# One-core gated cross-attention layer: projections' work redistributed over ScalarE, VectorE and GpSimd, k and q stored at full width, first groups' loads spread

## The chip, the cores and the metric

The kernel runs on one core of a Trainium2 chip. The metric is the device time of one execution in microseconds. The comparison is between medians of several executions; the profile is one execution of its own.

## The reference, cut to what matters

Eight sequences of 512 tokens with 256 features attend to a context of 512 tokens with 192 features, with 16 heads of 16; then an expert layer (8 experts, hidden size 1024) follows.

```
def layer(x, ctx):
    xn = (x - mean(x)) / sqrt(var(x) + 1e-5)            # per token, 256 features
    q = (xn @ Wq + bq) by heads;  k, v = (ctx @ Wk + bk), (ctx @ Wv + bv) by heads
    attn = softmax(clip(q k^T * 16**-0.5, -10000, 10000))
    x = x + tanh(g_xattn) * ((attn @ v) @ Wo + bo)
    xn = layernorm(x)
    gates = logits * (logits >= kth smallest),  logits = xn @ gate_weight.T
    return x + tanh(g_ffn) * sum over experts of gates[e] * (gelu(xn @ w1[e].T + b1[e]) @ w2[e].T + b2[e])
```

## The kernel before, in words

Three blocks of instructions follow each other; a block's engines start together, once all of them have finished the block before. The change touches the first, `build_project`, and the loads and matmul operands of the second, `build_attend`. The third, the experts, takes two thirds of the time and is not touched.

**Projections.** Each number that TensorE multiplies is split into a high part rounded to its short float32 format and a low part, and a product takes three matmuls (high by high, low by high, high by low). For each of the eight batches (of 512 tokens) x is normalised on VectorE (`layer_norm`, L392: statistics, small operations on 128x4 numbers, a square root on ScalarE, `root`, one Newton step, and at L401 the normalised x), transposed on TensorE (`turn`, L293), taken from PSUM by ScalarE (high part) and VectorE (low part, `split_x`, L419). GpSimd splits the weights (`split_weights`, L242, L245) and each batch's context (`split_ctx`, L251, L254). TensorE then makes k, q and v (L283); ScalarE and VectorE turn k and q into parts `k_hl` and `q_hl` (L354, L359, L410 to L414), 128 partitions x (part, half, 512) each, and ScalarE turns v into `v_out` (L365). Two buffers alternate by batch parity `p`. Every engine runs its own program in a fixed order, and semaphores tie them together.

**SyncE** issues every DMA of the block in one order. For each batch: the loads of x and ctxT two batches ahead (`load_x` L161, `load_ctx` L166), the stores of k and q (`store_qk`, L176), four of 256 KB each, and one store of v (`store_v`, L181, 544 KB). The k and q scratch has 33 rows for each head: a constant row, 16 high, 16 low. A store writes 16 rows of each of 8 heads, so its destination's dimensions are 8, 16, 512. After the sixth batch SyncE loads the q and k of groups 0 and 1 of batch 0 (`load_qk`, L443, eight DMAs a group, in pieces of 33 and 16, 17 and 32 rows), and then stores the last two batches. GpSimd fills all `q_st` and `k_st` tiles with 0 (L267, L268) before that.

**Attention.** A group is four heads of a batch; there are 32 groups. A head's q and k stand as 49 rows at the end of 64 partitions: constant row, and high and low parts in such an order that one matmul of 64 rows makes the three products. Scores of a group (L755) are reduced on VectorE to the least one of each row (L898), these lows are turned (L782), copied by ScalarE to `low_rows` (L1023) and sent by SyncE into the q tile's constant row (`send_lows`, L656). Then the transposed scores (L765) are made with that row, two groups later than the plain ones, exponentiated on ScalarE (L1012) and multiplied with v (L776). SyncE loads a group's q and k (`load_qk`) and v (L648) three groups ahead, each before the `send_lows` of the group after.

```
for name, tile, ready in (("k", k_hl[p], k_split), ("q", q_hl[p], q_split)):      # store_qk
    sp.wait_ge(ready, b + 1)
    rows = scratch[name][bass.ds(b, 1)].rearrange("a (k h r) t -> h r (a k) t", k=KT, r=KEPT)
```

## Time and profile before

| | |
|---|---|
| median of 3 runs | 2134.78 us (2133.43 to 2135.88) |
| profiled execution | 2128.79 us, of which its span, first to last instruction, is 2127.0 |
| mean granted TensorE clock | 0.969 of full |
| TensorE matmul busy | 1981.7 us, 93% of the span |
| VectorE, ScalarE, GpSimd busy | 1315.1, 720.6, 116.5 us |
| HBM read, written | 76.34 MB, 26.08 MB |

In the rows PE is TensorE, PEld its weight loads, DVE is VectorE, ACT ScalarE, POOL GpSimd, SPq the queue of SyncE, in which the entries are the issues of DMAs, not their transfers. Times are microseconds from the span's start. L283 is line 283 of the kernel. Matmul durations overlap, since they are pipelined.

### The profile page before, as it was taken

Reading aid. Unit: us, or ns where it says so; the run is one execution under the profiler, and the core shown is the slowest. Engines: PE = TensorE matmul, PEld = TensorE weight load, DVE = VectorE, ACT = ScalarE, POOL = GpSimd, SP = SyncE. Lnnn points to the kernel's source line nnn. Section 1 sums busy time; section 2 is a strip of 40 time slices with the busy share of each in tenths; the row PEclk is TensorE's granted clock in tenths of the full one; section 3 lists DMA queues with packets and bytes.
Section 4 is the critical chain, followed back from the end, with each engine's and each line's share of the span. In section 5 each row is a group of like instructions: output and inputs, shape, how many; then the busy total and the mean of one; then the engine's idle time right before and its main releaser. Section 6 shows DMA issues by size and latency. Waiting matters only on the chain.

```text
span 2127.0 us, 29692 instructions
## 1 busy us (share of the span) xinstructions
PE 1981.7 (93%) x9252; PEld 1433.7 (67%) x9252; DVE 1315.1 (62%) x2501; ACT 720.6 (34%) x1206; POOL 116.5 (5%) x199
## 2 busy tenths in 40 slices
PE   4748999999985999999999999999999999999998
PEld 4643333333334887788888888888888888888887
DVE  7748888888844667565555456456555555654544
ACT  2224766676661222222222222222222222222222
POOL 6300110011112000000000000000000000000000
PEclk9877999999996999999999999999999999999999
DMA  4763322222311001110110011001001000100111
GB/s 137 240 194 104 83 71 76 81 79 66 81 31 42 0 19 43 30 35 10 35 30 15 10 30 35 10 30 35 10 16 49 10 15 25 35 15 10 41 34 35
DMA packets 80071, 103.49 MB, mean 49 GB/s; under 512 B 25986, under 2 KB 44164, under 8 KB 80004
## 3 DMA queue, kind: packets, MB, share of 16 engines
q1 hardware_dynamic: 80004, 102.71, 16.5%
q8 instruction: 28, 0.46, 0.1%
q14 instruction: 39, 0.32, 0.1%
HBM read 76.34 MB, written 26.08 MB: 48 GB/s over the span
## 4 chain that ended last, share of the span: by engine, by line
PE 67%; DVE 1%; issue 0%; ACT 0%; DVEq 0%; ACTq 0%
PE ps_h L1821 34%; PE ps_y L1835 34%; DVE h_lo L2042 0%; DVE h_hi L2038 0%; DVE w_hi L1981 0%; DVE gated L2107 0%; DVE w_lo L1983 0%; DVE out_T_acc L2112 0%; ACT gelu L1941 0%; DVE w_lo L2150 0%; DVE gate L2053 0%; PE ps_h L1903 0%; DVEq L1990 0%; PE ps_h L1871 0%; DVEq L2176 0%
## 5 line engine op out<-in xcount | busy, mean ns | idle before, releaser
L1941 ACT ACTIVATE gelu<-ps_h,b 128x512 f32<-128x512 f32 x512 | 352.8, 689 | 1084.5 <-PE ps_h L1821 1003.4
L2038 DVE CAST h_hi<-gelu 128x512 fp32r<-128x512 f32 x512 | 221.0, 432 | 574.6 <-ACT gelu L1941 568.9
L1821 PE MATMUL ps_h<-x_hi,w_hi 128*128 (+1 forms) x1024 | 408.8, 399 | 10.5 <-DVE w_lo L1983 9.2
L1835 PE MATMUL ps_y<-h_hi,w_hi 128*128 128x512 f32 x1024 | 405.5, 396 | 6.0 <-DVE h_lo L2042 6.0
L1821 PE MATMUL ps_h<-x_lo,w_hi 128*128 (+1 forms) x1024 | 406.2, 397 | 0.0
L1821 PE MATMUL ps_h<-x_hi,w_lo 128*128 (+1 forms) x1024 | 405.8, 396 | 0.0
L1835 PE MATMUL ps_y<-h_hi,w_lo 128*128 128x512 f32 x1024 | 405.1, 396 | 0.0
L1835 PE MATMUL ps_y<-h_lo,w_hi 128*128 128x512 f32 x1024 | 404.8, 395 | 0.0
L2042 DVE TENSOR_TENSOR h_lo<-gelu,h_hi 128x512 fp32r<-128x512 f32 x512 | 357.3, 698 | 16.6
L898 DVE TENSOR_REDUCE low<-ps_s 128x1 f32<-128x512 f32 x512 | 322.0, 684 | 40.1 <-PE ps_s L755 38.0
L1012 ACT ACTIVATE probs_T<-ps_t 128x512 f32<-128x512 f32 x384 | 207.5, 598 | 102.6 <-PE ps_t L765 100.4
L1821 PEld LDWEIGHTS ps_h<-x_hi,w_hi 128*128 128x128 f32 x1024 | 193.1, 189 | 56.3 <-DVE w_lo L1983 9.0
L755 PE MATMUL ps_s<-k_st,q_st 64*128 64x512 f32 x512 | 207.3, 482 | 24.2 <-SPq L673 22.5
L1835 PEld LDWEIGHTS ps_y<-h_hi,w_hi 128*128 128x128 f32 x1024 | 192.7, 188 | 54.8 <-DVE h_lo L2042 6.9
L1821 PEld LDWEIGHTS ps_h<-x_hi,w_lo 128*128 128x128 f32 x1024 | 193.0, 188 | 46.7
L1821 PEld LDWEIGHTS ps_h<-x_lo,w_hi 128*128 128x128 f32 x1024 | 193.1, 189 | 46.3
L1835 PEld LDWEIGHTS ps_y<-h_hi,w_lo 128*128 128x128 f32 x1024 | 192.5, 188 | 46.9
L1835 PEld LDWEIGHTS ps_y<-h_lo,w_hi 128*128 128x128 f32 x1024 | 192.6, 188 | 45.3
L765 PE MATMUL ps_t<-q_st,k_st 64*128 64x512 f32 x512 | 191.1, 456 | 10.9 <-ACT probs_T L1012 7.8
L765 PEld LDWEIGHTS ps_t<-q_st,k_st 64*128 64x128 f32 x512 | 79.6, 188 | 135.7 <-ACT probs_T L1012 78.4
L755 PEld LDWEIGHTS ps_s<-k_st,q_st 64*128 64x128 f32 x512 | 85.4, 194 | 41.5 <-SPq L673 22.7
L776 PE MATMUL ps_o<-probs_T,v_st 128*17 128x512 f32 x768 | 104.3, 616 | 1.2 <-ACT probs_T L1012 1.2
(211 smaller groups left out, 1290.8 us busy)
## 6 DMA issues: line engine op xcount, KB each, us to landing
gate<-gates_scratch SPq DMA_DIRECT2D x64, 256.0 KB, 3.3
q_st<-q_scratch SPq DMA_DIRECT2D x64, 132.0 KB
k_scratch<-k_hl SPq DMA_DIRECT2D x32, 256.0 KB
q_scratch<-q_hl SPq DMA_DIRECT2D x32, 256.0 KB
k_st<-k_scratch SPq DMA_DIRECT2D x64, 128.0 KB
w_raw<-in_w1T SPq DMA_DIRECT2D x8, 1024.0 KB, 5.0
w_raw<-in_w2T SPq DMA_DIRECT2D x7, 1024.0 KB, 5.4
v_scratch<-v_out SPq DMA_DIRECT2D x8, 544.0 KB
```

Of the source, the lines that this page charges most:

```text
L755: pe.matmul(ps_s[BANK_OF[at]][:], q_st[g][rows, j // 2, t * P:(t + 1) * P], k_st[g][rows, j // 2, :], start=True, stop=True).then_inc(scor ...
L765: pe.matmul(ps_t[BANK_OF[at]][:], k_st[g][rows, j // 2, k * P:(k + 1) * P], q_st[g][rows, j // 2, :], start=True, stop=True).then_inc(t_in ...
L776: mm = pe.matmul(ps_o[32 * j:32 * j + VW, :], v_st[g][:, k, j, :], probs_T[k][:, j, :], start=(k == 0), stop=(k == TT - 1))
L898: dve.tensor_reduce(low[:, g % 2, column:column + 1], ps_s[BANK_OF[at]][:], AX_X, ALU.min).then_inc(low_done, 1)
L1012: act.activation(probs_T[k][:, j, :], ps_t[BANK_OF[(g * TT + k) * GROUP + j]][:], ACT.Exp, scale=-1.0).then_inc(exp_done, 1)
L1821: mm = pe.matmul(ps_h[:, j % RING, :], w[:, k, at], x[:, k, bass.ds(c * SEQ, SEQ)], start=(i == 0), stop=(i == len(parts) - 1))
L1835: mm = pe.matmul(ps_y[s][:, d, :], w[:, j, at], h[:, j % RING, :], start=(j == 0 and i == 0), stop=(j == HT - 1 and i == 2))
L1941: act.activation(gelu[:, j % GELUS, :], ps_h[:, j % RING, :], ACT.Gelu_apprx_tanh, bias=b1[p][:, j:j + 1]).then_inc(gelu_done, 1)
L2038: dve.tensor_copy(h_hi[:, j % RING, :], gelu[:, j % GELUS, :]).then_inc(h_hi_done, 1)
L2042: dve.tensor_tensor(h_lo[:, j % RING, :], gelu[:, j % GELUS, :], h_hi[:, j % RING, :].bitcast(F32), ALU.subtract).then_inc(h_ready, 1)
```

## The change

In the projections, the splits of weights and context move from GpSimd to ScalarE (high part) and VectorE (low part). The reciprocal root moves from VectorE and ScalarE to GpSimd, as the chain of small operations that the attention already has. VectorE's order changes: a batch's statistics are taken one batch earlier than its normalisation. q's high part is written straight from PSUM by ScalarE and its low part by VectorE, so `q_full` goes; the weights of q are scaled in their split. In the first batch TensorE makes k, then turns x, makes v and then q. Scratch for k and q becomes (batch, 128, 2, 2, 512), and each is stored with one DMA of 1 MB. The constant rows are no longer stored or loaded: the plain scores use 48 rows, the transposed ones 49, and the k tiles are filled with 1 (one each before the roots of batches 2 to 5), the q tiles not at all. A group's q and k are loaded in 12 DMAs of 16 rows (64 KB). The loads of groups 0 and 1 are made six at a time, behind the stores of batches 2 to 5. The loops of SyncE and GpSimd are unrolled.

```diff
+QK_PIECES = 12
...
-            def store_qk(bb, p):
+            def store(bb, p):
                 b = bb * 2 + p
                 for name, tile, ready in (("k", k_hl[p], k_split), ("q", q_hl[p], q_split)):
                     sp.wait_ge(ready, b + 1)
-                    rows = scratch[name][bass.ds(b, 1)].rearrange("a (k h r) t -> h r (a k) t", k=KT, r=KEPT)
-                    for part in range(2):
-                        for k in range(KT):
-                            sp.dma_start(rows[:, 1 + part * HDIM:1 + (part + 1) * HDIM, k], tile[:, part, k].bitcast(F32)).then_inc(stored[p], 16)
-
-            def store_v(bb, p):
-                b = bb * 2 + p
+                    sp.dma_start(scratch[name][bass.ds(b, 1)].rearrange("a p c m t -> (a p) (c m t)"),
+                                 tile[:].rearrange("p c m t -> p (c m t)").bitcast(F32)).then_inc(stored[p], 16)
                 sp.wait_ge(v_ready, b + 1)
                 sp.dma_start(scratch["v"][bass.ds(b, 1), :, :].rearrange("a p n -> p (a n)"),
                              v_out[p][:].rearrange("p t h w -> p (t h w)")).then_inc(stored[p], 16)
...
-            sp.wait_ge(fills_set, 2)
-            for i, name in enumerate(("q", "k")):
-                sp.dma_start(scratch[name].rearrange("b (h r) t -> (b h) r t", r=KEPT)[:, 0, :], const_rows[:, i, :]).then_inc(consts_moved, 16)
-            with sp.Fori(0, BATCH // 2 - 1) as bb:
-                for p in range(2):
-                    load_x(bb + 1, p)
-                    load_ctx(bb + 1, p)
-                    store_qk(bb, p)
-                    store_v(bb, p)
-
-            sp.wait_ge(fills_set, 3)
-            sp.wait_ge(consts_moved, 48)
-            sp.wait_ge(stored[0], STORES)
-            for g in range(FIRST_GROUPS):
-                load_qk(sp, scratch, keep, 0, g, first_loaded)
-            for p in range(2):
-                store_qk(BATCH // 2 - 1, p)
-                store_v(BATCH // 2 - 1, p)
-            sp.wait_ge(first_loaded, 128 * FIRST_GROUPS)
+            sp.dma_start(keep["wo"][:], io["Wo"].rearrange("(k p) n -> p k n", p=P)).then_inc(wo_loaded, 16)
+
+            def load_first(i):
+
+                g, name = i // 2, ("q", "k")[i % 2]
+                if i == 0:
+                    sp.wait_ge(stored[0], STORES)
+                if name == "k":
+                    sp.wait_ge(consts_set, 4 + g + 1)
+                load_rows(sp, scratch, keep, name, 0, g, first_loaded)
+
+            for b in range(BATCH):
+                if b + 2 < BATCH:
+                    load_x(b // 2 + 1, b % 2)
+                    load_ctx(b // 2 + 1, b % 2)
+                store(b // 2, b % 2)
+                if 2 <= b < 2 + 2 * FIRST_GROUPS:
+                    load_first(b - 2)
+            sp.wait_ge(wo_loaded, 16)
+            sp.wait_ge(first_loaded, QK_PIECES * 16 * FIRST_GROUPS)
...
-                pool.wait_ge(ctx_loaded[p], bb * 32 + 32)
-                wait(pool, v_in_psum, b - 1)
-                pool.tensor_tensor(ctx_hi[p][:], ctx_t[p][:], zero[:].rearrange("p (a b) -> p a b", a=1).to_broadcast([P, KT, SEQ]),
-                                   ALU.add).then_inc(ctx_split, 1)
-                pool.wait_ge(ctx_split, b * 2 + 1)
-                pool.tensor_tensor(ctx_lo[p][:], ctx_t[p][:], ctx_hi[p][:].bitcast(F32), ALU.subtract).then_inc(ctx_split, 1)
...
+                dev, diff, square, spread, var, first_root, root_2, scaled = (moments[:, i, :] for i in range(8))
+                done = b * 9
+                pool.wait_ge(stats_done, b + 1)
+                wait(pool, xn_ready, b - 1)
+                pool.tensor_tensor(diff, stats[:, :, 1], stats[:, :, 4], ALU.subtract)
...
+                pool.tensor_tensor(result, first_root, dev, ALU.add).then_inc(rstd_done, 1)
+
             for p in range(2):
                 pool.memset(v_out[p][:], 1.0).then_inc(ones_set, 1)
-            split_ctx(0, 1)
-            for i in range(2):
-                pool.memset(const_rows[:, i, :], float(i)).then_inc(fills_set, 1)
-
-            for s in range(GROUPS):
-                pool.memset(keep["q_st"][s][:].bitcast(F32), 0.0)
-                ins = pool.memset(keep["k_st"][s][:].bitcast(F32), 0.0)
-            ins.then_inc(fills_set, 1)
+            root(0, 0)
+            root(0, 1)
             pool.memset(keep["nan_flag"][:], 0)
-            with pool.Fori(1, BATCH // 2) as bb:
-                for p in range(2):
-                    split_ctx(bb, p)
+            for b in range(2, BATCH):
+                if b - 2 < GROUPS:
+                    pool.wait_ge(stats_done, b + 1)
+                    pool.memset(keep["k_st"][b - 2][:].bitcast(F32), 1.0).then_inc(consts_set, 1)
+                root(b // 2, b % 2)
...
+                    project_k(bb, p)
+                    if first:
+                        pe.wait_ge(ident_set, 2)
+                        turn(bb, p)
+                        values(bb, p)
+                    project_q(bb, p)
+                    if before_last(last, p, 1):
                         turn(bb + p, 1 - p)
-                    values(bb, p)
-
-            turn(0, 0)
+                    if not first:
...
+            def take_ctx(bb, p):
                 b = bb * 2 + p
-                act.wait_ge(stats_done, b * 4 + 4)
-                act.activation(std[:], meanvar[:, 1, :], ACT.Sqrt, bias=eps[:, 0:1]).then_inc(std_done, 1)
+                if isinstance(bb, int) and bb == 0:
+                    act.wait_ge(ones_set, p + 1)
+                act.wait_ge(ctx_loaded[p], bb * 32 + 32)
+                wait(act, v_in_psum, b - 1)
+                act.activation(ctx_hi[p][:], ctx_t[p][:], ACT.Copy).then_inc(ctx_hi_done, 1)
...
-                act.wait_ge(q_in_psum, b + 1)
-                wait(act, q_split, b)
-
+
+            def take_q(bb, p):
+                act.wait_ge(q_in_psum, bb * 2 + p + 1)
                 for m in range(KT):
-                    act.activation(q_full[:, m, :], ps_q[:, m, :], ACT.Identity, bias=bq_scaled[:, m:m + 1],
-                                   scale=-(HDIM ** -0.5)).then_inc(q_full_ready, 1)
+                    act.activation(q_hl[p][:, 0, m, :], ps_q[:, m, :], ACT.Identity, bias=bq_scaled[:, m:m + 1]).then_inc(q_hi_done, 1)
...
+            def statistics(bb, p):
                 b = bb * 2 + p
                 dve.wait_ge(x_loaded[p], bb * 16 + 16)
-                wait(dve, xn_ready, b)
-                mean_variance(dve, [x_t[p][:, t, :] for t in range(TT)], stats, meanvar, stats_done, b)
-                dve.wait_ge(std_done, b + 1)
-                rstd = reciprocal_root(dve, std[:], meanvar[:, 1, :], newton, newton_done, b)
+                wait(dve, rstd_done, b)
+                for t in range(TT):
+                    ins = dve.bn_stats(stats[:, t, :], x_t[p][:, t, :])
+                ins.then_inc(stats_done, 1)
+
+            def normalise(bb, p):
+                b = bb * 2 + p
+                dve.wait_ge(rstd_done, b + 1)
                 wait(dve, xT_in_psum, b - 1)
                 for t in range(TT):
-                    ins = dve.tensor_scalar(xn[p][:, t, :], x_t[p][:, t, :], meanvar[:, 0, t:t + 1], rstd[:, t:t + 1],
+                    ins = dve.tensor_scalar(xn[p][:, t, :], x_t[p][:, t, :], rstd[:, p, 0, t:t + 1], rstd[:, p, 1, t:t + 1],
                                             ALU.subtract, ALU.mult)
                 ins.then_inc(xn_ready, 1)
 
-            def take(bb, p):
+            def split_ctx(bb, p):
+                dve.wait_ge(ctx_hi_done, bb * 2 + p + 1)
+                dve.tensor_tensor(ctx_lo[p][:], ctx_t[p][:], ctx_hi[p][:].bitcast(F32), ALU.subtract).then_inc(ctx_split, 1)
+
+            def split_k(bb, p):
+                dve.wait_ge(k_hi_done, bb * 2 + p + 1)
+                dve.tensor_tensor(k_hl[p][:, 1], ps_k[:], k_hl[p][:, 0].bitcast(F32), ALU.subtract).then_inc(k_split, 1)
+
+            def split_q(bb, p):
                 b = bb * 2 + p
-                wait(dve, stored[p], bb * STORES)
-
-                dve.wait_ge(k_hi_done, b + 1)
-                dve.tensor_tensor(k_hl[p][:, 1], ps_k[:], k_hl[p][:, 0].bitcast(F32), ALU.subtract).then_inc(k_split, 1)
-                dve.wait_ge(q_full_ready, b * 2 + 2)
-                dve.tensor_copy(q_hl[p][:, 0], q_full[:]).then_inc(q_hi_done, 1)
-                dve.wait_ge(q_hi_done, b + 1)
-                dve.tensor_tensor(q_hl[p][:, 1], q_full[:], q_hl[p][:, 0].bitcast(F32), ALU.subtract).then_inc(q_split, 1)
+                for m in range(KT):
+                    dve.wait_ge(q_hi_done, b * 2 + m + 1)
+                    ins = dve.scalar_tensor_tensor(out=q_hl[p][:, 1, m, :], in0=ps_q[:, m, :], scalar=bq_scaled[:, m:m + 1],
+                                                   in1=q_hl[p][:, 0, m, :].bitcast(F32), op0=ALU.add, op1=ALU.subtract)
+                ins.then_inc(q_split, 1)
...
-                    if not (last and p == 1):
-                        layer_norm(bb + p, 1 - p)
-                    take(bb, p)
-                    if not (last and p == 1):
+                    first = isinstance(bb, int) and bb == 0 and p == 0
+                    more = before_last(last, p, 1)
+                    if first:
+                        split_k(bb, p)
+                        split_x(bb, p)
+                    if more:
+                        normalise(bb + p, 1 - p)
+                        split_ctx(bb + p, 1 - p)
+                    if first:
+                        dve.wait_ge(bq_ready, 1)
+                    else:
+                        split_k(bb, p)
+                    split_q(bb, p)
+                    if not last:
+                        statistics(bb + 1, p)
+                    if more:
                         split_x(bb + p, 1 - p)
 
-            layer_norm(0, 0)
-            split_x(0, 0)
+            statistics(0, 0)
+            split_weights(0, "wk", 1.0)
+            split_ctx(0, 0)
+            split_weights(1, "wq", -(HDIM ** -0.5))
+            split_weights(2, "wv", 1.0)
+            normalise(0, 0)
+            statistics(0, 1)
...
-    for name, dst, pieces in (("q", keep["q_st"][g], ((0, KEPT), (1, 1 + HDIM))),
-                              ("k", keep["k_st"][g], ((0, 1 + HDIM), (1, KEPT)))):
-        src = scratch[name][bass.ds(b, 1)].rearrange("a (g k h r) t -> (a g) h r k t", g=GROUPS, k=2, h=2)
-        for half in range(2):
-            row = half * 64 + 64 - ROWS
-            for lo, hi in pieces:
-                sp.dma_start(dst[row:row + hi - lo, :, :].bitcast(F32), src[g, half, lo:hi]).then_inc(loaded, 16)
-                row += hi - lo
+    for name in ("q", "k"):
+        load_rows(sp, scratch, keep, name, b, g, loaded)
+
+
+def load_rows(sp, scratch, keep, name, b, g, loaded):
+
+
+    dst, parts = {"q": (keep["q_st"][g], (0, 0, 1)), "k": (keep["k_st"][g], (0, 1, 0))}[name]
+    for half in range(2):
+        for i, part in enumerate(parts):
+            row = half * 64 + i * HDIM
+            sp.dma_start(dst[row:row + HDIM, :, :].bitcast(F32),
+                         qk_rows(scratch[name], b, g, half, part)).then_inc(loaded, 16)
+
+
+def qk_rows(rows, b, g, half, part):
+
+    return rows[bass.ds(b, 1)].rearrange("a (g k h r) c m t -> (a g) h m c r k t", g=2, k=2, h=2)[g % 2, half, g // 2, part]
...
-                    row = half * 64 + 64 - ROWS
+                    row = half * 64 + ROWS
...
-                rows = half_rows(j)
+                rows = half_rows(j, ROWS)
...
+                rows = half_rows(j, ROWS + 1)
...
-            "q": scratch_of("q_scratch", (BATCH, HEADS * KEPT, SEQ)),
-            "k": scratch_of("k_scratch", (BATCH, HEADS * KEPT, SEQ)),
+            "q": scratch_of("q_scratch", (BATCH, P, 2, KT, SEQ)),
+            "k": scratch_of("k_scratch", (BATCH, P, 2, KT, SEQ)),
```

## Rows read from the trace of the kernel before

**Rows 1.** The page's slices: TensorE's busy tenths in 40 parts of the span
```profile
PE   4748999999985999999999999999999999999998
```

**Rows 2.** TensorE's order of time (start, us, what, [idle before <-releaser]), attention's start
```profile
161.40 1.22 PE L755 MATMUL ps_s<-k_st,q_st 64*128 64x512 f32 x3 [22.54 <-SPq L673]
...
183.19 0.76 PE L765 MATMUL ps_t<-q_st,k_st 64*128 64x512 f32 x1 [0.95 <-DMA q_st<-low_rows]
```

**Rows 3.** SyncE's queue in order of time, one batch and the first groups' loads
```profile
76.25 0.97 SPq L181 DMA_DIRECT2D v_scratch<-v_out  x1
...
85.49 5.19 SPq L176 DMA_DIRECT2D q_scratch<-q_hl  x4
90.87 1.08 SPq L181 DMA_DIRECT2D v_scratch<-v_out  x1
...
121.43 3.66 SPq L443 DMA_DIRECT2D q_st<-q_scratch  x4
...
128.08 5.02 SPq L443 DMA_DIRECT2D k_st<-k_scratch  x4
```

**Rows 4.** Windows of 1 us: busy us by engine, TensorE's clock, DMA share, GB/s
```profile
144.00:145.00 1.00, 0.00 (x0) 0.00 (x0) 0.00 (x0) 0.00 (x0) 0.00 (x0) 0.50 0.52 201
...
147.00:148.00 1.00, 0.00 (x0) 0.00 (x0) 0.00 (x0) 0.00 (x0) 0.00 (x0) 0.50 0.98 350
...
159.00:160.00 1.00, 0.00 (x0) 0.00 (x0) 0.00 (x0) 0.00 (x0) 0.00 (x0) 0.50 0.48 150
```

**Rows 5.** VectorE and GpSimd in order of time, projections
```profile
4.85 1.41 DVE L452 BATCH_NORM_STATS2 stats_a<-x_t 128x6 f32<-128x256 f32 x4 [3.97 <-DMA x_t<-in_x]
...
14.71 9.54 DVE L401 TENSOR_SCALAR xn_a<-x_t,meanvar_a,newton_a 128x256 f32<-128x256 f32 x4
...
20.85 2.34 POOL L254 TENSOR_TENSOR ctx_lo<-ctx_t,ctx_hi 128x1024 fp32r<-128x1024 f32 x1
...
25.09 0.95 POOL L268 MEMSET k_st<- 128x1024 f32 x1
...
92.68 1.38 DVE L401 TENSOR_SCALAR xn_a<-x_t,meanvar_a,newton_a 128x256 f32<-128x256 f32 x4
93.97 1.22 DVE L410 TENSOR_TENSOR k_hl<-ps_k,k_hl 128x1024 fp32r<-128x1024 f32 x1
```

**Rows 6.** TensorE in order of time: last transposes, then first k, first v, last v
```profile
124.22 1.97 PE L293 MATMUL ps_x<-ident,xn_a 128*128 128x128 f32 x8 [4.25 <-DVE xn_a L401]
...
130.21 0.39 PE L283 MATMUL ps_k<-ctx_hi,wk_hi 128*128 128x512 f32 x1
...
135.82 0.28 PE L283 MATMUL ps_v<-wv_hi,ctx_hi 128*128 128x256 f32 x1
...
138.58 0.28 PE L283 MATMUL ps_v<-wv_hi,ctx_lo 128*128 128x256 f32 x1
```

**Rows 7.** GpSimd's root in the attention: first and last of 15 operations
```profile
256.39 0.21 POOL L712 TENSOR_TENSOR moments_b<-stats_b 128x4 f32<-128x4 f32 x1 [22.90 <-DVE stats_b L940]
...
260.72 0.20 POOL L736 TENSOR_TENSOR moments_b<-moments_b 128x4 f32<-128x4 f32 x1
```

**Rows 8.** SyncE's queue in the attention, one group and the next one's first loads
```profile
316.33 1.80 SPq L443 DMA_DIRECT2D q_st<-q_scratch  x4
...
319.80 0.62 SPq L648 DMA_DIRECT2D v_st<-v_scratch  x1
321.56 1.35 SPq L656 DMA_DIRECT2D q_st<-low_rows  x2
329.36 1.80 SPq L443 DMA_DIRECT2D q_st<-q_scratch  x4
```

**Rows 9.** TensorE in order of time, inside a group of the attention
```profile
302.05 0.50 PE L765 MATMUL ps_t<-q_st,k_st 64*128 64x512 f32 x1
...
302.05 0.73 PE L755 MATMUL ps_s<-k_st,q_st 64*128 64x512 f32 x2
...
302.71 1.05 PE L776 MATMUL ps_o<-probs_T,v_st 128*17 128x512 f32 x8
```

More of the change, by code:

```diff
@@ L154, in pairs, with before_last @@
             pair(BATCH // 2 - 1, True)
+        def before_last(last, p, ahead):
+            return not last or p + ahead < 2
         @block.sync
@@ L231, in _ @@
             pool.wait_ge(ones_set, 2)
+            for tile, value in ((exponent, -0.5), (quarter, 0.25), (half, 0.5), (one, 1.0)):
+                pool.memset(tile[:], value).then_inc(consts_set, 1)
             pool.memset(keep["ident"][:], 0.0).then_inc(ident_set, 1)
@@ L294, in turn, with project_k, project_q @@
                 mm.then_inc(xT_in_psum, 1)
-            def project(bb, p):
+            def project_k(bb, p):
+                b = bb * 2 + p
+                if isinstance(bb, int) and b == 0:
+                    pe.wait_ge(w_split, 1)
+                pe.wait_ge(ctx_split, b + 1)
+                wait(pe, k_split, b)
+                wk, ctx_parts = (w_hi["wk"], w_lo["wk"]), (ctx_hi[p], ctx_lo[p])
+                for m in range(KT):
+                    mm = product(ps_k[:, m, :], lambda a, k: wk[a][:, k, m * P:(m + 1) * P], lambda a, k: ctx_parts[a][:, k, :])
+                mm.then_inc(k_in_psum, 1)
+            def project_q(bb, p):
                 b = bb * 2 + p
@@ L299, in project @@
                     pe.wait_ge(w_split, 2)
[L300 to L308 removed]
                 pe.wait_ge(xT_ready, b + 1)
[L310 removed]
+                wait(pe, q_split, b)
+                wq, xn_parts = (w_hi["wq"], w_lo["wq"]), (xn_hi, xn_lo)
                 for m in range(KT):
@@ L422, in pair @@
                 for p in range(2):
-                    if not (last and p == 1):
-                        layer_norm(bb + p, 1 - p)
-                    take(bb, p)
-                    if not (last and p == 1):
-                        split_x(bb + p, 1 - p)
-            layer_norm(0, 0)
-            split_x(0, 0)
+                    first = isinstance(bb, int) and bb == 0 and p == 0
+                    more = before_last(last, p, 1)
+                    if first:
+                        split_k(bb, p)
+                        split_x(bb, p)
```

150 lines of the change are left out of this document (76 added, 74 removed).

## The prediction

> **What bounds the kernel now.** I first read the page's slices: from the fifth on TensorE is busy 9 tenths or just under, and the change has nothing there but loads; in the first four it is busy 4 to 8 tenths [rows 1]. TensorE's order of time gives the size of that part. The attention's first score comes at 161.40, after a wait of 22.54 us for SyncE, and the first transposed score at 183.19 [rows 2]. So the projections fill 161.4 us of 2127.0, and from there on the kernel takes 1965.6.
>
> Next the SyncE queue for one batch. From one v store to the next is 76.25 to 90.87, 14.6 us, and four q stores of 256 KB take 5.19 us merely to be issued [rows 3]: the issues wait for the transfers ahead. Windows of 1 us tell why. While only q stores run, DMA moves 201 GB/s at a busy share of 0.52, half of the 16 engines; when the v store runs it moves 350 GB/s at 0.98 [rows 4]. The k and q destinations have 8 heads as their slowest dimension, v's has 128 partitions. By the shapes a batch stores 2.10 MB of k and q (10.4 us at 201) and 0.56 of v, and loads 0.52 of x and 0.39 of ctxT (1.47 MB, 4.2 us at 350): 14.6 us, the period seen. The stage is bound by half-width stores. Its ends are bound otherwise: the first TensorE work comes at 24.4, as normalising took 9.54 us beside GpSimd's work, against 1.38 with GpSimd idle [rows 5]; and at the end SyncE issues the loads of groups 0 and 1 from 121.4 to 133.1 ahead of the last two batches' stores [rows 3], so the block ends 22.5 us after the last projection.
>
> **The change, part by part.** *Stores.* One DMA of 1 MB for k and one for q, 128 partitions wide, 8 KB each. The nearest row is v's store, 350 GB/s [rows 4]. A batch then needs 3.57 / 0.35 = 10.2 us of DMA, and with one of the new sixfold loads (0.39 MB) 11.3. Nothing in the rows excludes that HBM takes writes no faster than 201 GB/s; that is the lower bound and a rival.
>
> *Engines.* With DMA at 10.2 something else decides. TensorE needs for k and q 24 matmuls (130.21 to 135.82, 5.6 us), for v 24 (135.82 to 138.86, 3.0), and about 1.0 for 8 transposes, at full clock 9.6 us; after a wait of some 4 us it ran slower, 6.0 instead of 4.0 for transposes and values [rows 6]. VectorE has statistics 1.4, normalise 1.38, and 1.22 for each of ctx, k and x (the row of k's low half); q comes in two halves of 512, between 1.22 (the same elements) and 1.5 (my value, for a second start): 8.0 us [rows 5]. ScalarE is below that, with five such passes of about 1.0 us. None fills 12 us, but three make a ring. Statistics(b+2) stand late in VectorE's iteration b; GpSimd then fills a k_st (0.95 [rows 5]) and takes the root; VectorE's next iteration begins with normalise(b+2), which waits for it. The same 15 small GpSimd operations stand in the attention, 256.39 to 260.92, 4.53 us [rows 7]. The ring: statistics 1.4, fill 0.95, root 4.53, normalise 1.38, ctx 1.22, k 1.22, q 1.5, two hand-overs at 0.1: **12.4 us**, and 11.45 where nothing is filled (batches 6 and 7). The split of x hides in the root's time. Today's stalls, like the 9.54 us, go with GpSimd's passes over whole tiles, such as ctx_lo of 2.34 [rows 5].
>
> The Trainium skill (SBUF — State Buffer, the shared port pair) says that a VectorE operation in a two-port mode, or one with two SBUF inputs against a GpSimd operation that reads SBUF, blocks the other or is blocked for the whole instruction. The trace agrees (9.54 us). By that rule the splits of weights and ctx, now on VectorE, could meet root(0) and lose about their own 0.7 to 1.2 us once; in the ring they do not meet a root.
>
> *Is x there in time?* Set the end of statistics(b+2) to 0; normalise(b+2) ends at +7.0, the k and q splits at +9.5 and +11. The same points of the turn before are k's store at -2.9 and q's at -1.4. Normalise(b+1) ended at -5.4; transposes and values take 4.0 to 6.0, v_out 1.2, so v's store goes at -0.2 to +1.8. Its 2.66 MB with k and q are through the queue at about +5; for b = 2 to 4 six loads follow (1.1 us of transfer), then x (1.5), then the completion, about 2.6 us (the first load, issued as the kernel begins, had landed by 4.85 [rows 5]: about 4.1 in all, 1.5 of it transfer): x(b+3) lands at +9.1, or +10.2 with the loads. Statistics(b+3) want it at +11. Margin 0.8 to 1.9: with DMA somewhat fuller it is gone. For three batches I add 0.7 each, 2 us.
>
> *Start.* SyncE waits for two more memsets, about 1 us; ctxT is issued by 4.8 and lands by 8.9 (4.1 as the first load). ScalarE's hi 1.0, VectorE's lo 1.22, hand-overs: first matmul at 11.4 instead of 24.4. k(0) at the lower clock, twice 2.8, to 17.0; transposes 1.2 and values 3.0 to 21.2; q(0) to 24.1, its two halves on ScalarE and VectorE to 26.2; statistics(2) end at 27.6.
>
> *Stage.* From 27.6 four turns of 12.4 and one of 11.45 to statistics(7): 88.7, late x 2: 90.7; root and normalise 6.0: 96.7; from the last transposes to the end of the last values 14.6 (124.22 to 138.86 [rows 6]), v_out 1.2, its store's issue 1.0, the block's end 0.4: **113.9**. Saved: 161.4 - 113.9 = **47.5 us**. The first groups' loads ride in the ring. Also gone, with no further gain: the square roots' table loads and half of the fills, which other work hides, and two 256 KB constant stores.
>
> *Attention.* From 161.4 to 183.19 VectorE reduces 32 scores, then TensorE waits 0.95 for low_rows [rows 2]. The work is the same after; a quicker landing may give that 0.95 back, four more loads ahead of low_rows may take as much: 0. In each later group SyncE issues 12 loads instead of 8. At 1.80 for four [rows 8] that is 1.8 us more; v_st and the low rows stand behind. v_st's issue ends at 320.42 and the rows go at 321.56, slack 1.1: they go 0.7 later. The matmuls that want them start at the group's end, which releases the next loads at 329.36 [rows 8], 6.4 us after the rows' issue. Covered: 0, within +-1. Without that cover it would be 0.7 x 30 = 21 us.
>
> The Trainium skill (DMA: Bandwidth & Descriptors, Rules for kernel authors) speaks against this piece: coalesce, under 64 KB a transfer is mostly overhead, and these are 64 KB. In the rows the overhead is hidden; by the rule alone the loads would cost those 0.7 a group.
>
> The matmuls take 48 or 49 rows instead of 64; their time goes by columns if the pairing stays (rival 4). Nothing behind the attention changes.
>
> **The sum.** The profiled execution is 2128.8 (its span 2127.0); less 47.5 it is 2081.3. The median of runs is 6.0 above it, so 2134.8 - 47.5 = **2087.3**.
>
> **Rivals.**
> (1) DMA is the ring after all. For: from a first store at 19 us on, 21.3 MB of stores, 5.5 of loads and 1.6 for the first groups are 28.4 MB in 95 us, 299 GB/s, not far under 350. Against: the margin above, and 350 seen. A turn of 13.2 to 14.5 instead of 12.4, six times: 5 to 13 us more, 2092 to 2100.
> (2) Better: x is in time, q's halves cost 1.22, the start comes earlier. 2 + 5 x 0.3 + up to 4: 2 to 8 us less, 2079 to 2085.
> (3) The stores gain nothing, HBM writes stay at 201 GB/s. For: one window late in the stage has only 150 at a share of 0.48; against: v's 350 [rows 4]. The period stays 14.6, and only the start (18 us) and the loads' place (7) count: 2110.
> (4) The other side. In the attention a score and a transposed score, each on 64 rows, one from partition 0 and one from 64, start together (302.05) [rows 9]. If 48 and 49 rows were not placed so, every pair would be serial: at 0.234 for 512 columns (5.6 / 24) 512 x 0.234 = 120 us more on TensorE, less at most the tenth of some 450 us that it is idle there [rows 1]: +75, net +27: 2162. It decides when some three pairs in four fall apart. Against: eight matmuls of 17 columns take 1.05 us [rows 9] where one behind another would take 1.9, so an odd width is placed side by side.
>
> **How the numbers follow.** Forecast 0.60; (1) 0.19; (2) 0.14; (3) 0.03; (4) 0.02; no net change for a reason not listed 0.02. 0.2% (4.3 us) is about what a measurement of this kernel can tell from no change. Faster 0.95, same 0.02, slower 0.03. The forecast's own range is 2083 to 2092; to hold 8 in 10 it reaches into (1) and (2): 2078 to 2100.
>
> **What would show it.** First matmul near 11.4, v stores 12.4 apart, first score near 114; DMA near 350 GB/s in the k and q stores; normalise released by GpSimd's root some 5.5 us after each statistics; scores and transposed scores still starting in pairs; 21 to 22 us from the first score to the first transposed one. I am wrong if statistics wait for x (DMA is the ring), if TensorE stays at the lower clock through whole batches (some 17 us of work), or if low_rows hold TensorE more often than now.

## The result and the profile after

The changed kernel takes 2076.05 us (median of four, 2071.11 to 2078.57) against 2134.11 for the kernel before (four runs, 2127.24 to 2135.88): a recorded ratio of 0.9721, 95% interval 0.9704 to 0.9739 (the two medians divided give 0.9728). That is 11.2 us under the forecast of 2087.3 and 2 under the range of 2078 to 2100. The profiled execution took 2074.38, its span is 2072.6.

The slices of the page of the kernel after, TensorE, its granted clock and DMA, answer to [rows 1]:

```profile
PE   7899999999958999999999999999999999999998
PEclk9979999999969999999999999999999999999999
DMA  7832222222110010000010010001010001000100
```

TensorE is filled from the third slice on instead of the fifth. Its order of time says when the projections begin and end (a row: start us, us, engine, line, operation, count, the idle time ahead and what ended it), as [rows 2] did for before:

```profile
9.88 0.77 PE L285 MATMUL ps_k<-ctx_hi,wk_hi 128*128 128x512 f32 x1 [9.88 <-DVE ctx_lo L435]
...
105.40 0.82 PE L814 MATMUL ps_s<-k_st,q_st 48*128 48x512 f32 x3 [2.00 <-SPq L732]
...
125.44 0.62 PE L824 MATMUL ps_t<-q_st,k_st 49*128 49x512 f32 x1
125.53 1.30 PE L814 MATMUL ps_s<-k_st,q_st 48*128 48x512 f32 x2
...
617.42 0.76 PE L1878 MATMUL ps_h<-x_hi,w_hi 128*128 128x512 f32 x1 [8.76 <-DVE w_lo L2040]
```

First score 105.40 instead of 161.40: the stage gives 56.0 us where 47.5 were forecast. Between there and the end 1.6 go back: 1967.2 instead of 1965.6. First score to first transposed score takes 20.0 instead of 21.8 (the wait of 0.95 for low_rows is gone, and VectorE's first reduction starts 0.7 us behind the first score instead of 1.3); from there to the experts' first matmul it is 492.0 instead of 488.3 (671.52 less 183.19); the experts differ by 0.3.

One turn of VectorE in the stage, which the forecast laid out as a ring, in order of time:

```profile
24.61 1.40 DVE L421 BATCH_NORM_STATS2 stats_a<-x_t 128x6 f32<-128x256 f32 x4
25.92 1.21 DVE L452 TENSOR_TENSOR xn_lo<-ps_x,xn_hi 128x1024 fp32r<-128x1024 f32 x1
31.51 1.38 DVE L429 TENSOR_SCALAR xn_a<-x_t,rstd_a 128x256 f32<-128x256 f32 x4 [4.38 <-POOL rstd_a L266]
32.81 1.22 DVE L435 TENSOR_TENSOR ctx_lo<-ctx_t,ctx_hi 128x1024 fp32r<-128x1024 f32 x1
33.94 1.22 DVE L439 TENSOR_TENSOR k_hl<-ps_k,k_hl 128x1024 fp32r<-128x1024 f32 x1
35.08 1.40 DVE L445 SCALAR_TENSOR_TENSOR q_hl<-ps_q,bq_scaled,q_hl 128x512 fp32r<-128x512 f32 x2
36.39 1.39 DVE L421 BATCH_NORM_STATS2 stats_a<-x_t 128x6 f32<-128x256 f32 x4
```

and GpSimd's part of it, between statistics and normalise:

```profile
26.06 0.95 POOL L276 MEMSET k_st<- 128x1024 f32 x1 [6.20 <-DVE stats_a L421]
26.98 0.20 POOL L242 TENSOR_TENSOR moments_a<-stats_a 128x4 f32<-128x4 f32 x1
...
31.27 0.20 POOL L266 TENSOR_TENSOR rstd_a<-moments_a 128x4 f32<-128x4 f32 x1
```

The ring is as it was drawn, and takes 11.78 us, not 12.4. What ended VectorE's idle time ahead of the two ends of the ring in the whole stage (line L429, then L421; us, times):

```profile
  POOL rstd_a L266: 26.8, 8
...
  DMA x_t<-in_x: 5.4, 2
```

Normalise waits for the root eight times of eight. Statistics wait for x twice, 4.76 for the first load and 0.65 in batch 7.

### The profile page after: what moved, and what is told of

It is laid out like the page before. It is cut to its first block, busy times and chain, and to the rows that moved or that the text cites. A ratio compares the mean times of both kernels' runs of the same rounds, so it can differ in the third digit from the quotient of the medians.

```text
span 2072.6 us, 29677 instructions
## 1 busy us (share of the span) xinstructions
PE 1978.3 (95%) x9252; PEld 1426.3 (69%) x9252; DVE 1271.3 (61%) x2415; ACT 725.1 (35%) x1206; POOL 102.0 (5%) x294
## 4 chain that ended last, share of the span: by engine, by line
PE 69%; DVE 1%; ACT 0%; issue 0%; DVEq 0%; ACTq 0%
PE ps_h L1878 35%; PE ps_y L1892 35%; DVE h_lo L2099 0%; DVE h_hi L2095 0%; ACT gelu L1998 0%; DVE gated L2164 0%; ACT L1998 0%; DVE out_T_acc L2169 0%; DVE w_lo L2040 0%; DVE w_lo L2207 0%; DVE w_hi L2038 0%; PE ps_h L1960 0%; PE ps_h L1928 0%; DVEq L2233 0%; DVEq L2094 0%
## 5 line engine op out<-in xcount | busy, mean ns | idle before, releaser
L814 PE MATMUL ps_s<-k_st,q_st 48*128 48x512 f32 x512 | 209.9, 488 | 3.2 <-SPq L732 2.0
L824 PE MATMUL ps_t<-q_st,k_st 49*128 49x512 f32 x512 | 194.0, 463 | 9.3 <-ACT probs_T L1071 7.9
L824 PEld LDWEIGHTS ps_t<-q_st,k_st 49*128 49x128 f32 x512 | 81.0, 191 | 134.9 <-ACT probs_T L1071 76.5
L814 PEld LDWEIGHTS ps_s<-k_st,q_st 48*128 48x128 f32 x512 | 86.6, 196 | 20.4 <-DVE low L957 15.7
```

The lines of the kernel that those rows point to most:

```text
L814: pe.matmul(ps_s[BANK_OF[at]][:], q_st[g][rows, j // 2, t * P:(t + 1) * P], k_st[g][rows, j // 2, :], start=True, stop=True).then_inc(scor ...
L824: pe.matmul(ps_t[BANK_OF[at]][:], k_st[g][rows, j // 2, k * P:(k + 1) * P], q_st[g][rows, j // 2, :], start=True, stop=True).then_inc(t_in ...
```

## The experiments

Each kernel is the changed one with the edit shown, unless something else is said; each was executed once, but for the two of the version that beats both. They are read by the time of the first score (105.4 after, 161.4 before), since the stages behind it differ from one execution to the next by more than some of the edits are worth: among thirteen traces with the new attention the time from the first score to the end lies between 1963.8 and 1968.7.

### The changes to transfers alone

The kernel before, with the new layout of scratch, full-width stores, twelve loads a group and 48 or 49 rows; its engines keep their work, and the first groups' loads their place.

```diff
-rows = scratch[name][...].rearrange("a (k h r) t -> h r (a k) t", ...)
-for part, k: sp.dma_start(rows[:, 1 + part * HDIM:1 + (part + 1) * HDIM, k], tile[:, part, k])
+sp.dma_start(scratch[name][...].rearrange("a p c m t -> (a p) (c m t)"), tile[:])
```

> The kernel before with only the storage part of the change: new scratch, k and q stored in one full-width DMA each, no constant rows, 12 loads a group (at the old place), 48 and 49 rows. GpSimd still splits, VectorE still takes the roots. If half-width stores were the bound before, the turn falls from 14.6 to what VectorE with its stalls needs, 12 to 13.5; the start stays (first matmul 24.4), the end loses its 20 us of store issues but keeps the first loads, now some 5 to 8 us: first score at 126 to 138 instead of 161.4, so 25 to 35 of the 56 us. The rest, 20 to 30 us, would then belong to the start (14) and to the shorter turn.

First score 133.12, execution 2103.61: 28.3 of the 56.0 us. The starts of statistics 1 and 7 (28.58 and 115.50 before, 35.33 and 108.22 here, 13.84 and 83.60 after) cut the stage in three:

```profile
35.33 1.39 DVE L452 BATCH_NORM_STATS2 stats_a<-x_t 128x6 f32<-128x256 f32 x4
...
108.22 1.40 DVE L452 BATCH_NORM_STATS2 stats_a<-x_t 128x6 f32<-128x256 f32 x4
...
133.12 0.72 PE L755 MATMUL ps_s<-k_st,q_st 48*128 48x512 f32 x3 [1.94 <-SPq L673]
```

| stretch, us | before | transfers alone | after |
|---|---|---|---|
| to the start of statistics(1) | 28.6 | 35.3 | 13.8 |
| six turns | 86.9 | 72.9 | 69.8 |
| statistics(7) to first score | 45.9 | 24.9 | 21.8 |

The transfers alone bring 14.0 of the 17.2 us gained in the turns and 21.0 of the 24.1 behind statistics(7). At the start they bring nothing. There this run is 6.8 us slower than before (first matmul 31.16 instead of 24.40, where I had expected 24.4), because normalise(0) takes 15.79 us instead of 9.54 (and starts 0.5 later). The last of its four instructions, begun at 21.34 together with GpSimd's ctx_lo, ends at 31.01, 0.2 behind the last of the eight fills that follow:

```profile
15.22 15.79 DVE L392 TENSOR_SCALAR xn_a<-x_t,meanvar_a,newton_a 128x256 f32<-128x256 f32 x4
...
23.62 0.95 POOL L258 MEMSET q_st<- 128x1024 f32 x1
...
29.87 0.95 POOL L259 MEMSET k_st<- 128x1024 f32 x1
```

Before, two shorter fills of the constant rows stood ahead of the eight, and the same instruction ended at 24.26; why it got through there and not here is not shown. So 28.3 understates the transfers: without this collision they would be worth about 35 us (an estimate, 28.3 plus 6.8). The rest of the change (work moved between engines, the order of statistics, the spread of the first loads) gives 27.7 us over this run, 21.5 of it at the start; against the kernel before the start gained 14.7.

### How wide the stores are

Four stores instead of one, first written with the 8 heads slowest, then with 128 partitions:

```diff
+rows = scratch[name][...].rearrange("a (h r) c m t -> h r (a c) m t", r=HDIM)
+for c, m: sp.dma_start(rows[:, :, c, m], tile[:, c, m])
```

> The changed kernel, but k and q are stored as before: four DMAs each whose slowest destination dimension is the 8 heads. If the width of the stores is what the change lives on (half of the DMA engines at 201 GB/s), a batch costs DMA 2.10/0.201 + 1.47/0.35 = 14.6 us, with a sixfold load 15.8, against a ring of VectorE and GpSimd of 11.8; seven turns add 20 to 27 us and the last batch's issues some 5 to 8 more: the first score comes at 130 to 140 instead of 105.4, the span is 2098 to 2108. Rival, the engines' redistribution did it: first score at 105 to 109, span about 2074.

> The changed kernel, but k and q are stored in four DMAs of 256 KB each, all of them 128 partitions wide (2 KB pieces). If width alone counts, the stage is as in the changed kernel, first score within 1.5 us of 105.4. Rival, the larger piece (8 KB) or the smaller number of DMAs counts: first score 3 to 20 us later, with DMA's GB/s in the store windows well under the 350 and more of the changed kernel.

First scores 107.14 and 106.42, executions 2076.64 and 2076.42. The first kernel was meant to be half as wide, and wasn't. Its windows while the stores run (the last three columns are granted clock, DMA share, GB/s) show it:

```profile
36.00:37.00 1.00, 1.00 (x8) 0.88 (x7) 1.00 (x5) 0.49 (x1) 0.00 (x0) 1.00 1.04 371
37.00:38.00 1.00, 1.00 (x6) 0.80 (x5) 1.00 (x3) 1.00 (x2) 0.57 (x1) 1.00 1.08 334
```

and its first score, in TensorE's order of time:

```profile
107.14 1.22 PE L816 MATMUL ps_s<-k_st,q_st 48*128 48x512 f32 x3 [2.56 <-SPq L734]
```

```diff
-"q": scratch_of("q_scratch", (BATCH, P, 2, KT, SEQ)),
+"q": scratch_of("q_scratch", (BATCH, P // HDIM * (HDIM + 1), 2, KT, SEQ)),
+rows = scratch[name][...].rearrange("a (h r) c m t -> h r (a c) m t", r=HDIM + 1)
+for c, m: sp.dma_start(rows[:, :HDIM, c, m], tile[:, c, m])
```

> The changed kernel with its k and q stores made eight wide in fact: the scratch keeps 17 rows for a head of 16, so that heads and rows can't be read as one dimension of 128, and each part is written by its own 256 KB store with the 8 heads slowest, as the kernel before did. Theory A (width is what the stores gain by): the k and q stores run near 201 GB/s at a share near 0.52, a turn is 14.6 us, 15.7 with six loads in it, against 11.8; statistics wait for x in every turn and the first score comes at 122 to 130 instead of 105.4; execution 2091 to 2099. Theory B (loads beside the stores fill the other half of the engines, so width is not needed): turns stay at 11.8 to 12.5, first score 105 to 109, execution 2074 to 2080.

While q is stored (windows with SyncE alone, so clock, share and GB/s again stand last), the DMA share is half, as before [rows 4]; the stage's mean from 24 to 105 is 228 GB/s:

```profile
42.00:43.00 1.00, 1.00 0.52 195
43.00:44.00 1.00, 1.00 0.52 201
...
24.00:105.00 81.00, 0.91 0.69 228
```

VectorE and TensorE of the same kernel in order of time:

```profile
87.47 1.41 DVE L423 BATCH_NORM_STATS2 stats_a<-x_t 128x6 f32<-128x256 f32 x4 [5.74 <-DMA x_t<-in_x]
...
104.36 1.40 DVE L423 BATCH_NORM_STATS2 stats_a<-x_t 128x6 f32<-128x256 f32 x4 [5.81 <-DMA x_t<-in_x]
...
142.47 1.22 PE L816 MATMUL ps_s<-k_st,q_st 48*128 48x512 f32 x3 [18.29 <-SPq L734]
```

First score 142.47, execution 2110.11. Statistics wait 3.9 to 5.8 us for x in every turn from batch 4 on, and those turns are 15.9 to 17.6; the last stores hold TensorE up for 18.3 us. The cause is theory A's; the size was missed (122 to 130), since I had given the loads 350 GB/s and forgotten the queue behind the last turn: 38.1 us from statistics(7) to the first score instead of 21.8. From the first kernel this one differs by the unused row alone, so half width costs 35.3 us in the new arrangement (142.47 less 107.14; against the single stores of the changed kernel it is 37.1). With half-width stores, the rest of the change brings 18.9 of the 56.0 us (161.40 less 142.47), and the transfers without the rest brought 28.3: neither alone gives all of it.

The Trainium skill (DMA: Bandwidth & Descriptors, the rule on the number of engines under "Why a DMA increments its semaphore by 16 and not by 1") says that a transfer gets the largest number of engines up to 16 that divides the slowest dimension of both sides. The traces agree, 0.52 for 8 heads and over 1.0 for 128, if the slowest dimension is taken after neighbouring ones have been merged, as the first kernel shows.

### Are the first groups' loads in the way?

```diff
-if 2 <= b < 2 + 2 * FIRST_GROUPS:
-    load_first(b - 2)
+if b == 5:
+    for i in range(2 * FIRST_GROUPS): load_first(i)
```

> The changed kernel, with all 24 loads of groups 0 and 1 made in one place behind the store of batch 5, not six at a time behind batches 2 to 5. Sum: they are 1.57 MB, 4.5 us at 350 GB/s, and their issue blocks SyncE for up to 20 us (5 us for six in the changed kernel), while batch 6's stores wait behind; the stores of batches 6 and 7 then leave later: first score 3 to 10 us later than 105.4. Rival, DMA has slack enough near the end: within 1 us.

Behind the first load statistics never wait for x now, and statistics(7) start at 82.97 instead of 83.60; the first score comes at 105.27. The 0.6 us are given back behind the 24 loads. The execution took 2072.10, 2.3 less, but that difference lies behind the first score (1965.0 instead of 1967.2), where nothing was changed. The loads' place is worth nothing here.

### The fill in the ring

The fill of k_st behind the root; then behind the root and behind a wait for normalise:

```diff
 for b in range(2, BATCH):
+    root(b // 2, b % 2)
     if b - 2 < GROUPS:
-        pool.wait_ge(stats_done, b + 1)
+        pool.wait_ge(xn_ready, b + 1)      # this line in the second kernel only
         pool.memset(keep["k_st"][b - 2][:].bitcast(F32), 1.0)...
-    root(b // 2, b % 2)
```

> The changed kernel, with each fill of a k tile (0.95 us) put behind GpSimd's root instead of ahead of it, so that it starts when VectorE starts to normalise. Ring theory: the four turns with a fill shrink by what the fill stood in them: 11.8 to 10.9, first score 3.5 to 4 us earlier, about 101.7. If the fill and the normalising (SBUF to SBUF) hold each other up, up to 0.95 of it comes back in each turn, and normalise takes up to 2.3 instead of 1.38: first score near 105. Rival, DMA bounds the turn: no gain although normalise stays at 1.38.

> As the run before, but the fill also waits until VectorE has normalised, so that the two don't meet. Ring theory: first score 3.5 to 4 us earlier than 105.4, turns of 10.9, unless x arrives too late: in the changed kernel its last late batch waited 0.65, so up to 1 us of the gain may go into waits of statistics for x. Rival, DMA bounds: first score at 104.5 or later.

Turns of 11.48 and 10.9 instead of 11.8, first scores 103.17 and 101.48, executions 2073.00 and 2067.07. The fill takes its own 0.9 us in the ring, as costed. Put right behind the root, 0.1 us before normalise starts, it lengthens normalise by 0.6 instead, as VectorE's order of time in the first kernel shows:

```profile
30.46 1.95 DVE L428 TENSOR_SCALAR xn_a<-x_t,rstd_a 128x256 f32<-128x256 f32 x4 [3.50 <-POOL rstd_a L266]
32.34 1.21 DVE L434 TENSOR_TENSOR ctx_lo<-ctx_t,ctx_hi 128x1024 fp32r<-128x1024 f32 x1
```

and in the second:

```profile
30.21 1.38 DVE L429 TENSOR_SCALAR xn_a<-x_t,rstd_a 128x256 f32<-128x256 f32 x4 [3.50 <-POOL rstd_a L266]
31.50 1.22 DVE L435 TENSOR_TENSOR ctx_lo<-ctx_t,ctx_hi 128x1024 fp32r<-128x1024 f32 x1
```

The Trainium skill (SBUF — State Buffer, Who interferes with whom) says that tensor_scalar can run in a two-port mode and then contends with any GpSimd instruction, the later one blocked in full. The rows agree that they contend (1.95 us instead of 1.38), but not that the loss is the whole of the overlap: normalise loses 0.57 of the 0.84 us that the fill still had to run. Against the eight fills in a row of the run with the transfers alone it did wait for the last one.

### Statistics and x earlier

With the fill as in the second kernel above, statistics right behind normalise, ahead of the three splits; then the same with x of batch b+3 issued behind k's store of batch b, as its tile is free from normalise(b+1) on, where after issues it behind v's store:

```diff
 normalise(bb + p, 1 - p)
+statistics(bb + 1, p)
 split_ctx(bb + p, 1 - p); split_k(bb, p); split_q(bb, p)
-statistics(bb + 1, p)
```
```diff
 store_part(b, "k", ...)
+load_x((b + 3) // 2, (b + 3) % 2)          # second kernel only
 store_part(b, "q", ...)
```

> The run before plus another order on VectorE: statistics(b+2) right behind normalise(b+1), ahead of the splits of ctx, k and q, so that GpSimd's root lies beside 5 us of splits. The ring of 10.9 then loses those 3.9 us and bounds no longer (7.3); TensorE (9.6) or DMA (10.2, 11.3 with a sixfold load) would, were x there. But x(b+2) was issued only behind v's store and behind the sixfold loads, so VectorE waits for it with its splits queued behind: I expect waits of statistics for x of 1 to 4 us a turn, turns between 10.5 and 13, first score at 98 to 108.

> The run before plus another order on SyncE: x(b+3) is loaded right behind k's store of batch b, ctx(b+3) behind v's, ahead of the sixfold loads. With x in time neither the ring nor x bounds: turns of 10.2 to 11.3 (DMA) or 9.6 to 10.5 (TensorE), first score at 93 to 99. If the run before gains as much, x was not late; if this one has turns near 11.8 too, the ring was not the bound.

The first is 18 us worse than after: first score 123.71, execution 2091.87. From batch 3 on statistics wait for x 5.4 to 8.3 us in every turn, and the splits queued behind them wait too, so their stores come late, and x behind the stores:

```profile
54.02 1.21 DVE L452 TENSOR_TENSOR xn_lo<-ps_x,xn_hi 128x1024 fp32r<-128x1024 f32 x1
56.13 1.38 DVE L429 TENSOR_SCALAR xn_a<-x_t,rstd_a 128x256 f32<-128x256 f32 x4 [0.90 <-POOL rstd_a L266]
65.80 1.41 DVE L421 BATCH_NORM_STATS2 stats_a<-x_t 128x6 f32<-128x256 f32 x4 [8.29 <-DMA x_t<-in_x]
```

I had expected the waits, but of 1 to 4 us and with a first score at 98 to 108; what I had not seen is that loop. With x early the first score comes at 95.91, execution 2063.85; statistics still wait 2.0, 2.1, 3.8 and 2.3.

### A version that beats both

x ahead of k's store too; then also the first groups' loads behind batch 5's stores. Medians of four executions each, against 2131.96 for before (seven).

```diff
 for b in range(BATCH):
+    load_x((b + 3) // 2, (b + 3) % 2)
     store_part(b, "k", ...)
-    load_x((b + 3) // 2, (b + 3) % 2)
```

> As the run with statistics and x early (first score 95.9, execution 2063.9, statistics waiting 2.0, 2.1, 3.8 and 2.3 us for x), with one more step: x of batch b+3 is issued ahead of k's store instead of behind it, so it is not queued behind 1 MB. Theory A (the place of x in the queue makes the waits): the waits for x go or fall below 0.5 us, turns fall to about 9.8 to 10.5, first score 89 to 93, execution 2057 to 2061. Theory B (the DMA engines are full, so that whatever goes first, something else comes late): the wait moves to ctx or to a store's buffer, first score 94 to 97, execution 2062 to 2065.

> As the run before, and the 24 loads of the first groups all behind batch 5's stores instead of six behind each of batches 2 to 5. Theory A: 1.6 MB leave the turns of batches 2 to 4 (1.1 us each) and come where DMA has less to do; if DMA is the ring the first score comes 2 to 3 us before that of the run above; execution 1 to 3 us less. Theory B: the stores of batches 6 and 7 stand behind 24 issues (some 10 us, as in the kernel before's 133.1 minus 121.4) and the last v store, with the end of the stage, comes later than above by 1 to 5 us.

2061.75 (2060.50 to 2063.83), ratio 0.9668 (0.9647 to 0.9689), first score 95.03; and 2059.94 (2058.25 to 2062.09), ratio 0.9659 (0.9637 to 0.9680), first score 91.75. In the first, turns are 8.2 to 8.4 until statistics(5), and then x is late again, by 4.05 and 3.18, where it stands in the queue behind the stores and the sixfold loads. A window over its stage (the length, each engine's busy time and instructions, then clock, DMA share and GB/s) says why:

```profile
26.00:95.00 69.00, 64.44 (x375) 55.81 (x373) 46.36 (x78) 33.47 (x39) 28.07 (x87) 0.98 1.04 365
```

and the second kernel's:

```profile
26.00:92.00 66.00, 63.02 (x378) 55.06 (x377) 46.70 (x79) 33.84 (x39) 28.77 (x88) 1.00 0.97 357
```

DMA is full from end to end in the first kernel. That is theory B, whose 94 to 97 for the first score held; its place for the wait did not, since it is still x that is late. Theory A holds for the second, 3.3 us earlier, whose loads stand where DMA had room. Here DMA has become the ring, as rival (1) had it. TensorE is not far behind: it is busy for 64.4 of 69 us in the first and for 63.0 of 66 in the second. In the changed kernel itself DMA was not the ring:

```profile
19.00:106.00 87.00, 73.65 (x407) 62.26 (x407) 52.86 (x91) 37.74 (x44) 27.00 (x107) 0.96 0.84 309
```

### The attention's 3.7 us

The kernel before again, unchanged; and the changed kernel, which from batch 1 on leaves out four of a group's twelve loads (the third product uses rows of another group).

```diff
-for i, part in enumerate(parts):
+for i, part in enumerate(parts[:2] if later else parts):
```

> The kernel before, unchanged, for a second trace. Theory A (the attention of the changed kernel is longer by its loads): first transposed score to the experts' first matmul again 488.3 within 1. Theory B (such lengths differ from execution to execution with the places of the low-clock stretches, as 489.6 to 492.9 among ten traces of the new attention): a value off 488.3 by more than 1, up to 493.

> The changed kernel; from batch 1 on a group in the attention loads 8 of its 12 pieces of q and k (the third product, low q by high k, is left with rows of another group). Theory A (the four more loads cost 0.1 us a group): first transposed score to the experts 488.3 to 489. Theory B (they are hidden): 489.6 to 493 as in the ten traces with 12 loads, and an undisturbed batch stays at 57.1 us between loads of x_res.

From the first transposed score to the experts: 488.04 in before again, 490.83 with eight loads. So 488.3 was no accident, and the loads are not what is longer. An undisturbed batch is the same in both, 57.07 us from one load of x_res to the next before (337.19 less 280.12), 57.09 after:

```profile
224.47 0.40 SPq L729 DMA_DIRECT2D x_res<-in_x  x1
...
281.56 0.40 SPq L729 DMA_DIRECT2D x_res<-in_x  x1
```

What differs is TensorE's clock. A window over that whole stretch, TensorE alone (length, busy us, clock, share, GB/s), of before:

```profile
183.19:671.52 488.33, 431.05 (x2594) 0.95 0.24 67
```

and of after:

```profile
125.44:617.42 491.98, 436.92 (x2594) 0.94 0.23 65
```

The same 2594 matmuls are busy for 5.9 us more. Adding up the stretches granted half the clock (1.2 instead of 2.4 GHz) gives 48.0 and 47.7 us in the two traces of before, 61.9 in after, 57.3 with eight loads. Over the thirteen traces with the new attention the length follows them: 489.6 where they are 52.6 (two traces), 490.4 to 491.1 where they are 56.9 to 57.6 (five), 492.0 to 492.9 where they are 59.1 to 62.8 (six). That is 0.3 us for each us at half clock, and carried on to 48 it gives 488.2, the length of before. Why the new attention has 5 to 15 us more at half the clock was not found; no experiment held the clock fixed, so this is an agreement of numbers and not a shown cause. A rival stays untested: all thirteen traces have scores on 48 and 49 rows instead of 64, and no run has the new transfers with the old rows.

## Why the prediction was wrong

Its mechanism was right: the stage turned into the ring of VectorE and GpSimd that it drew, and DMA was not the bound. What failed are terms of its sum, the same way in all but one. By size they are the step from the profiled execution to the median (4.3 us), the tail (2.8), the turns (2.7), the start (1.6) and late x (1.35); the attention missed by 1.9 the other way. The steps of the stage, forecast and measured:

| step | forecast | after | gained more |
|---|---|---|---|
| statistics(2) end | 27.6 | 26.0 | 1.6 |
| five turns and late x, to the end of statistics(7) | 63.1 | 59.0 | 4.1 |
| root and normalise | 6.0 | 6.0 | 0 |
| transposes to first score | 17.2 | 14.4 | 2.8 |
| first score | 113.9 | 105.4 | 8.5 |

*The turn*. Full turns measured 11.8 where 12.4 was summed, four times 0.6, and the short one 11.07 instead of 11.45. The sum added durations, but a VectorE operation starts 0.08 to 0.10 us before the one ahead has ended: 31.51 plus 1.38 is 32.89, and the next starts at 32.81. [Rows 5] show that already (92.68 plus 1.38, next at 93.97). Four such joints on VectorE and one of 0.03 on GpSimd are 0.37; the hand-overs took 0.09 instead of 0.2, the root 4.49 instead of 4.53, and q's halves 1.40 instead of 1.5: 0.6 in all. *Late x*, 2.0 for three batches, was 0.65 in one. The two are 4.1 us. The margin of x was sized with 350 GB/s for the stores, and they ran faster (410, below): x(4) landed at 45.28, 7.5 us behind the end of statistics(3), where +9.1 was forecast.

*The start*: first matmul 9.88 instead of 11.4, as ctx_lo started at 8.51 where I had ctxT's landing alone at 8.9 (it was issued by 4.21 instead of 4.8 and took 3.1 instead of 4.1); that is 1.5 of the 1.6. The collision that the prediction feared for root(0) did happen, without holding TensorE up: beside ctx_lo its operation at 8.69 took 1.93 us, against 1.01 for the same one in root(7).

*The tail*: for transposes to values I took 14.6 from [rows 6], and those hold a stretch at half clock (granted 0.83 from 124.22 to 138.86). In after the clock was full there: 12.4, and 0.6 less for v_out and block end.

*Outside the stage.* The attention was costed at 0 within 1 and takes 1.9 more (20.0 instead of 21.8 ahead of it, 492.0 instead of 488.3 in it); the loads are not the cause, and the cause stays open. It was luck that this went against the other errors. *The medians*: the 6.0 by which before's median lies above its profiled execution were carried over, and after's lies 1.7 above. That term has no mechanism behind it: before's profiled execution, 2128.79, lay below all three of its runs. The 4.3 us are more than the 2 by which the range was missed. 8.5 less 1.6, plus 4.3, are the 11.2 us by which the median was missed.

*The rivals.* (1) did not come true in the changed kernel (share 0.84), but DMA is the ring in the version whose stage is 10.4 us shorter. (2) was the nearest and stopped 3 us short of the result: x was nearly in time and the start came earlier, but q's halves took 1.40 and not 1.22. (3) is refuted by what DMA moves from 36 to 42, where only stores run (length, then clock, share, GB/s):

```profile
36.00:42.00 6.00, 0.86 1.02 410
```

The prediction's sentence that nothing in the rows excludes writes at 201 GB/s at most was wrong already by the v store's 350 [rows 4]. That the kernel with 17 rows a head took 2110.11, just what (3) gives, is what half-width stores cost and no limit of HBM; (3)'s 18 us for the start had no rows either, and 14.7 were measured. (4) is refuted too: transposed scores and scores of 49 and 48 rows start together inside a group (301.36, against 302.05 of [rows 9]):

```profile
301.36 0.49 PE L824 MATMUL ps_t<-q_st,k_st 49*128 49x512 f32 x1
301.36 0.72 PE L814 MATMUL ps_s<-k_st,q_st 48*128 48x512 f32 x2
```

The claim that the old stalls go with GpSimd's passes held. They matter at the start, which gained 14.7 us, and hardly in the turns, where all that is not transfers gave 3.1. The Trainium skill (DMA: Bandwidth & Descriptors, Rules for kernel authors) advises against transfers under 64 KB, and the prediction put 0.7 us a group on that rule. No run here agrees: leaving out a third of the 64 KB loads brought nothing beyond the spread.

## What to carry to other kernels

Lay a stage out as rings through the in-order engines and cost each by start-to-start distances of consecutive rows, not by a sum of durations plus hand-overs: errors of 0.1 us with one sign add up over every joint and turn. Do not carry the distance between one profiled execution and the median over to another kernel. Before an operation is moved ahead in an in-order engine, ask if its input is there, since a wait moves everything behind it, and what is behind it may be what brings the input. When one ring is shortened, look at what the others have left: here DMA was full once the stage was 10.4 us shorter, and TensorE was busy for 63.0 of 66 us once it was 13.7 shorter.

## What the runs showed that was not expected

A store written with 8 heads slowest ran at a DMA share of 1.04 and 1.08 when the heads' rows lay without gap, and at 0.52 with one unused row in 17 (35.3 us for that row). Stores moved more than the 350 GB/s of the best row of before shown: 410 as a mean over 6 us of stores alone, and 365 as a mean over 69 us for stores and loads together. One GpSimd memset of 0.95 us beside a VectorE normalisation lengthened it from 1.38 to 1.95; a split and eight such fills in a row held one of its instructions for 9.67 us, which takes 0.41 alone.
